# Moving the bias products of a mixture-of-experts layer from among its tiles to behind the last tile

## The reference

```python
logits = einsum('btd,ed->bte', x, router_w) + router_b
topk_val, topk_idx = top_k(logits, 2)
cw = einsum('btk,btke->bte', softmax(topk_val), one_hot(topk_idx, 8))
h1, h2 = split(einsum('btd,efd->btef', x, fc1_w) + fc1_b, 2)
y = einsum('bteh,edh->bted', silu(h1) * h2, fc2_w) + fc2_b
out = einsum('bted,bte->btd', y, cw)          # added to the residual h
```

## Time and profile before

| | us |
|---|---|
| median of 3 runs | 165.27 |
| the three runs | 165.27, 163.89, 165.62 |
| the profiled execution, its own time | 165.16 |
| its span in the profile | 163.4 |
| busy in the span: PE, DVE, ACT, POOL | 113.8 (70%), 114.9 (70%), 73.4 (45%), 94.9 (58%) |

### The profile page before, as it was taken

How to read it: one execution, slowest core, us unless ns; L and a number is a source line. 1 busy time by engine, 2 the same in 40 slices (tenths; PEclk the granted TensorE clock), 3 DMA queues, 4 the chain that set the end, 5 groups by cost and what they waited for, 6 DMA issues and landing times.

```text
span 163.4 us, 3439 instructions
## 1 busy us (share of the span) xinstructions
PE 113.8 (70%) x764; PEld 96.7 (59%) x764; DVE 114.9 (70%) x479; ACT 73.4 (45%) x236; POOL 94.9 (58%) x114
## 2 busy tenths in 40 slices
PE   0001867349879858569999899999999999990000
PEld 0000446229648438457997799897789999980000
DVE  1899674899599999686275776676677888750183
ACT  3032851045654060176153567675566777760000
POOL 4778779100278777277237777777764667765000
PEclk9999999975899965555559999999999999999555
DMA  4311223970072441144133114433431101110894
GB/s 113 110 48 38 50 57 88 179 268 0 4 220 75 130 163 39 51 111 114 36 96 99 49 53 115 118 99 114 102 81 33 40 21 48 50 47 0 269 366 135
DMA packets 15077, 15.65 MB, mean 96 GB/s; under 512 B 2979, under 2 KB 11685, under 8 KB 15058
## 3 DMA queue, kind: packets, MB, share of 16 engines
q1 hardware_dynamic: 10210, 8.25, 20.0%
q0 software_dynamic: 2784, 5.28, 10.0%
q10 hardware_dynamic: 2064, 1.90, 3.4%
HBM read 9.62 MB, written 6.27 MB: 97 GB/s over the span
## 4 chain that ended last, share of the span: by engine, by line
PE 24%; issue 10%; POOL 7%; DVE 5%; DMA 5%; DVEq 1%; ACTq 1%; POOLq 0%; ACT 0%
POOL results L365 7%; PE bank L1178 6%; PE bank L1164 6%; PE bank L1154 5%; DMA yres<-results 4%; PE bank L1196 3%; PE bank L1144 2%; DMA results<-ysb,dest 1%; PE bank L1046 1%; DVEq L711 1%; PE bank L1023 1%; DVE act_h L725 1%; DVE ysum L820 1%; DVE res L823 1%; ACTq L973 1%
## 5 line engine op out<-in xcount | busy, mean ns | idle before, releaser
L354 POOL DMA_INDIRECT sorted_rows<-rows,slot x32 | 33.2, 1037 | 26.9 <-DVE slot L627 18.1
L714 DVE COPY w1b<-w_sb 128x516 f32 x39 | 19.9, 511 | 12.2 <-DVE act_h L725 4.9
L365 POOL DMA_INDIRECT results<-ysb,dest x22 | 21.6, 981 | 11.4 <-issue 8.7
L725 DVE SCALAR_TENSOR_TENSOR act_h<-bank,w1b,sil 128x128 f32<-128x128 f32 x78 | 23.5, 341 | 4.9 <-PE bank L1164 2.0
L1164 PE MATMUL bank<-xT,w1b 128*128 128x128 f32 x156 | 25.8, 292 | 0.7 <-DVE act_h L725 0.7
L1178 PE MATMUL bank<-w_sb,act_h 128*128 x156 | 25.6, 288 | 0.7 <-issue 0.4
L1154 PE MATMUL bank<-xT,w1b 128*128 128x128 f32 x156 | 25.6, 290 | 0.0
L926 ACT ACTIVATE sil<-bank,w1b 128x128 f32<-128x128 f32 x78 | 24.3, 363 | 0.6 <-PE bank L1154 0.6
L917 ACT COPY xT<-bank 128x128 f32<-128x128 f32 x39 | 10.3, 264 | 29.7 <-PE bank L1144 29.7
L365 POOL DMA_INDIRECT results<-ysb,xt x17 | 17.7, 1041 | 9.8 <-ACT ysb L946 7.6
L1164 PEld LDWEIGHTS bank<-xT,w1b 128*128 128x128 f32 x156 | 22.3, 207 | 1.0 <-DVE act_h L725 1.0
(11 more groups left out here) (234 smaller groups left out, 185.8 us busy)
## 6 DMA issues: line engine op xcount, KB each, us to landing
w_sb<-w_all SPq DMA_DIRECT2D x8, 386.0 KB, 5.4
xt<-sorted_rows SPq DMA_DIRECT2D x39, 65.0 KB, 1.9
yres<-results SPq DMA_DIRECT2D x4, 256.0 KB, 4.6
yres<-results ACTq DMA_DIRECT2D x4, 256.0 KB, 5.2
sorted_rows<-pad SPq DMA_DIRECT2D x1, 520.0 KB, 6.1
sorted_rows<-rows,slot POOLq DMA_INDIRECT x32, 2.6
out<-res SPq DMA_DIRECT2D x2, 256.0 KB, 2.8
out<-res ACTq DMA_DIRECT2D x2, 256.0 KB, 2.4
```

The lines of the kernel that those rows point to most:

```text
L354: gp.indirect_dma_start(sorted_rows[:, :], bass.IndirectOffsetOnAxis(ap=slot[:, k, t:t + 1], axis=0), rows[:, k, t, :], None).then_inc(s_s ...
L365: gp.indirect_dma_start(results[:, :], bass.IndirectOffsetOnAxis(ap=target, axis=0), ysb[i][:, :], None, bounds_check=bound, oob_is_err=Fa ...
L714: v.tensor_copy(w1b[i % 4][:, :], w_sb[:, bass.ds(at, W1)]).then_inc(s_wb, 1)
L725: v.scalar_tensor_tensor(act_h[i % 2][:, q], ps_l[sides(i)][:, q], w1b[i % 4][:, 2 * HID + 2 + c:2 * HID + 3 + c], sil[i % 2][:, q], ALU.a ...
```

## The change

The four products and the four additions leave the tiles. PE makes all four products behind `second(38)`, and DVE makes all four additions behind the last tile and ahead of the final sums. The products alternate between two banks, bank 0 and bank 6: product 1 waits for the last copy out of bank 6 (`s_te` at 39), products 2 and 3 wait for the addition two groups earlier (`s_added` at g - 1). Number and form of the instructions stay as they were.

```diff
-ADD_AT = [12, 15, 18, 21]
...
-        ps_add = banks[0]
+        ps_add = [banks[0], banks[6]]
...
-                v.tensor_tensor(e, e, ps_add[:, :], ALU.add).then_inc(s_added, 1)
+                v.tensor_tensor(e, e, ps_add[g % 2][:, :], ALU.add).then_inc(s_added, 1)
...
-                if i - 1 in ADD_AT:
-                    add_bias(ADD_AT.index(i - 1))
-
+
+            for g in range(NG):
+                add_bias(g)
             for g in range(NG):
                 dve.wait_ge(s_yl[g], 32)
                 dve.wait_ge(s_added, g + 1)
...
-                if g >= 1:
-                    pe.wait_ge(s_added, g)
-                te.matmul(ps_add[:, :], mixT[:, g, :], bias_d[:, :, :].rearrange("p j d -> p (j d)"),
+                if g == 1:
+                    pe.wait_ge(s_te, NTILES)
+                if g >= 2:
+                    pe.wait_ge(s_added, g - 1)
+                te.matmul(ps_add[g % 2][:, :], mixT[:, g, :], bias_d[:, :, :].rearrange("p j d -> p (j d)"),
...
-                if i in ADD_AT:
-                    mixed_bias(ADD_AT.index(i))
+            for g in range(NG):
+                mixed_bias(g)
```

## The result

The version with products and additions behind the last tile takes 160.47 us (median of 4 runs, 159.16 to 161.09) against 165.44 us (median of 4 runs of the kernel before, 163.89 to 167.05): a ratio of 0.970 with a 95% interval of 0.9625 to 0.977. The profiled execution took 160.59 us, with a span of 158.9. The forecast was 160.7 us.

A forecast was written before the change was run, and what follows sets the result against it. The prediction took POOL's own pace as the bound up to tile 17, PE's from tile 18 to 38, then the tail. Profiled 165.16 - 4.80 (products) + 0.3 (POOL), additions and tail 0, gave 160.7 us; range 159.4 to 163.2.

The forecast's parts named there:

- A product costs PE 1.20 us: Among the tiles on PE: each product costs 1.05 us plus 0.15 for restarting the transpose; four are 4.80 us.
- The additions cost nothing among the tiles: On DVE in the tiles: removing four additions of 0.69 us gains nothing, since DVE waits for PE there.
- POOL's pace decides how much of it comes through: POOL's scatters in the tiles: last one starts at 144.25, 4.5 us sooner, out of the 4.80 us PE gains.
- Both paces: POOL's time per scatter in the tiles: 1.29 us undisturbed, 1.45 us when disturbed by DVE's weight copy.
- meeting the copies again: POOL in the tiles: after nine free tiles scatters are tied until the next `weigh`; at most 0.65 us, taken as 0.3.
- Rival (A), POOL tied: POOL's scatters stay tied to DVE's copies at 1.449 us: 163.5 us, chance 0.14; tied in part, 161 to 163, 0.12.
- Rival (B), products at the lower clock: In the tail: four products at 1.2 GHz take about 8.4 us, last addition 1.5 us late: 162.2 us, chance 0.04.
- Rival (C), DVE as the bound: In tiles 13 to 35: 23 copies slowed by 0.25 us each on DVE, 5.8 us: 166.5 us, slower, chance 0.03.
- The tail's cover: Behind the last tile: last addition ends at 147.3, first final sum starts at 150.0; cover 2.7 us, cost 0.

The follow-up runs named there:

- the quiet traces: Profiles of the kernel before at 165 us and of the changed kernel at 160 us, without the 1 to 2 us standstills of PE, ACT and DVE.
- the probe: Changed kernel with back-to-back POOL scatters beside steady DVE copies added behind the output, run with copies every 1.26 us and every 1.43 us; total time of no interest.
- the moved version's later run: The changed kernel run again without an edit, where the kernel before took 187.0 us: 184.74 us, ratio 0.9895.
- a late start: Changed kernel with the four products held until all scatters have landed: 188.46 us, ratio 1.0135 against the kernel before.
- the later runs: All follow-up runs, on three chips, with tiles interrupted by standstills; the kernel before took 184 to 191 us there, the changed kernel 184.74 us, ratio 0.9895.
- the first probe: Changed kernel with 2 x 24 POOL scatters beside DVE copies added behind the output; copies every 1.26 us: none blocked in the first half, five in the second.
- the added measurement: Changed kernel with 2 x 24 POOL scatters beside DVE copies behind the output, copies every 1.428 us: twenty scatters in a row tied at that beat.

## Why the prediction was right

**A product costs PE 1.20 us.** Shown in the quiet traces (2.65 to 1.45 us between tiles 11 and 12, 4.81 us from tile 11 to 38). With products in other tiles the long distances moved with them (2.65 and 2.66 against 1.45 us). Over all interrupted tiles four cost some 2.5 us by one pair of traces and 0.8 by another, which the prediction had no case for.

**The additions cost nothing among the tiles.** Shown by leaving them out: ratio 1.005 with the products still there, 0.9915 with the products gone.

**POOL's pace decides how much of it comes through.** Both paces are in the trace after, and the forecast of 144.25 for the last scatter came out at 144.28, but not by the sum that gave it. The sum went by POOL: five scatters tied at 1.45 us, the others at 1.287, and 0.3 us for meeting the copies again. Only one was tied, because the `weigh` of tile 13 already shifts the copy (by 0.13 us: 106.32 against 104.74 + 1.45 = 106.19), and the scatter at 106.33, 0.01 behind it, passed. I had counted only the chunks with targets, from tile 17 on. And meeting the copies again cost nothing: at 116.63 and 128.23 a scatter started 0.29 us behind a copy, and both times a `weigh` (of tiles 21 and 29) stood ahead of the next copy and made it late, so that the next scatter began ahead of it (117.93 against 118.32, 129.53 against 129.56). That is luck of the places where `weigh` stands. So POOL by its own pace would have been at 104.88 + 1.45 + 29 x 1.287 = 143.65, and it caught up with ACT at tile 32, where it began to wait. From there PE's pace set the end, as it did before: ACT's result of tile 35 came 4.46 us sooner, and the last scatter 4.45. The 0.3 us that the sum added for POOL came to nothing, and the whole 4.80 us of PE came through; the 0.35 us by which tile 8 and all behind it started later in this execution fill the gap (143.93 + 0.35 = 144.28). Two errors cancel, and that the last scatter came within 0.03 us is luck; the term itself was right to 0.3 us. In tiles 32 to 35 POOL waited 0.6 us more than its 0.30 each, so a few more tied scatters would have cost nothing.

**Rival (A), POOL tied.** It didn't happen in this kernel, and the mechanism under it is shown by itself: twenty scatters in a row. The kernel gets free by a few hundredths of a microsecond, so another instruction between `act_h` and the copy, or one less, could decide 3 us; that was not shown in the kernel. The Trainium skill's rule ("SBUF — State Buffer", "Who interferes with whom"), a lock for the whole instruction, taken by the rows from the copy's start to its end, would have kept it tied. Measured is 0.30 us of a copy of 0.43, in the probe's scatters behind a copy too. That is a measure between starts and ends as the profile gives them: a scatter that needs nothing in its first 0.13 us and then waits for the copy's end would, where it is blocked, show the same ends, so no row tells when the lock itself ends.

**Rival (B), products at the lower clock.** It was nearer than its 0.04. In the quiet trace the clock was 0.90 in the last 1.1 us of the products, in the moved version's later run they took 5.21 us in place of 3.94, and with one bank or with twice the products the clock fell in the midst of them. My evidence was the 3.5 us at 1.00 behind PE's stop; that PE is busy in the tail was taken for a reason that the clock stays, and it is none. Before the change the clock fell 3.8 us behind the last matmul of the tiles with PE idle, and it fell 3.8 us behind it with the products there, so nothing in these two traces says that the products kept it up: in the quiet run they were over in time, and how near that was is in part luck. The price was too high, since it took four products by themselves: at 1.2 GHz the four took 7.19 us, not 8.4, 2.1 for the first and 1.71 for each behind it.

**Rival (C), DVE as the bound.** PE was busy for 34.00 of the 34.00 us from 105 to 139 in the quiet trace, so no gap of PE ahead of line 1177; it plays no part.

**The tail's cover.** 2.7 us were worked out, 2.72 stand in the trace, and 1.52 in the later run of the same kernel, where products were slower. Two details were off and cancelled: four products took 3.94 us and not 4.20, and the two banks did leave PE a wait, for product 2 starts at about 144.6, behind the end of addition 0 at 143.81 + 0.69 = 144.50, and not at 144.48. One bank, eight products or a late start go beyond the cover and cost time.

**What stays open:** why the kernels ran 20 us slower in the later runs, and why the change brought 2.2 us there and not 4.8. The standing still of DVE in the first probe is not a wait for another engine; what it is, no row shows.

## What to carry to other kernels

Work on the bound engine that nothing needs until the end belongs behind the last tile, if the engines that make and take it would be idle there: compare its length with the wait that it goes under, at the lower clock too. Ask of the next engine in the chain whether it can use the time: read its own pace (here 1.29 us by an idle time that is always 0.30) and where its backlog ends. Two engines that block each other in a fixed beat can tie themselves to each other, and removing a step may then make the beat steadier and the tie permanent (shown in the added measurement, not in the kernel). A piece measured by itself is not what the same work costs in a row.

## What the runs showed of the hardware

- A scatter issued by POOL that starts 0.05 to 0.24 us behind the start of a DVE copy of 128x516 float32 (0.43 us) ends as if it had started 0.30 us behind it. Scatters that started 0.01 or 0.03 us behind passed, and the copy took 0.48 us.
- With copies every 1.428 us, back-to-back scatters (1.28 us alone) lock to that beat after four and stay for the 20 that were left.
- The granted clock fell from 1.00 to 0.50 under matmuls of 32 rows by 512 columns that kept PE busy without a gap: by the shares of the stretches some 2.4 us after the first product where each was made twice, and 2.5 and 3.8 us after it in the two traces of the moved version. With PE idle it fell 3.8 us behind the last matmul of the kernel before. Products one at a time among the tiles left it at 1.00.
- At the lower clock such a product takes 1.71 us against 0.86 where it follows another, and 2.05 against 1.10 by itself: a factor of 2 and of 1.9.
